# Reordering the edges of a four-stage transformer kernel: weight splits, block boundaries and bank choices

## What is computed

```python
x = x + tanh(g_xattn[0]) * autocorrelation(layernorm(x), ctx, ctx)
x = x + tanh(g_ffn[0]) * lora_ffn(layernorm(x), W, b, A, B, gate_w, gate_b)
x = x + tanh(g_xattn[1]) * attention(layernorm(x), ctx, ctx, mask, wq, wk, wv, wo)
x = x + tanh(g_ffn[1]) * fourier_ffn(layernorm(x), W_base, b_base, enc, coefs, masks)
```

## Time and profile before

| | us |
|---|---|
| median of 3 runs | 3214.91 |
| lowest, highest | 3212.25, 3221.15 |
| the profiled execution, its own time | 3212.81 |
| its span in the trace | 3211.0 |
| TensorE busy in it | 3102.6 |
| VectorE, ScalarE, GpSimd busy | 1940.2, 1136.7, 711.4 |

### The profile page before, as it was taken

One profiled execution on the slowest core, in us unless ns is written; L12 is line 12 of the kernel. 1 busy time (PEld: TensorE's weight loads), 2 busy tenths in 40 slices (PEclk: granted clock), 3 DMA queues, 4 the chain that ended last, 5 costly groups with the idle time before them and its releaser, 6 DMA issues.

```text
span 3211.0 us, 42556 instructions
## 1 busy us (share of the span) xinstructions
PE 3102.6 (97%) x15200; PEld 2594.9 (81%) x15200; DVE 1940.2 (60%) x4647; ACT 1136.7 (35%) x2381; POOL 711.4 (22%) x580
## 2 busy tenths in 40 slices
PE   8999999998899999999999999899999899999999
PEld 7888788886677788887788888788888788888787
DVE  4333487786453577777666667566667566666432
ACT  4111466664222344444333333333333333333221
POOL 2422388884212233332100000000000000000131
PEclk9999999998999999999999999999999999999999
DMA  7332422204352577677564455364455354443621
GB/s 237 128 122 92 153 54 73 71 29 152 112 192 97 189 237 235 224 254 251 175 230 159 152 186 180 120 222 158 158 190 176 126 208 168 163 166 111 255 88 57
DMA packets 232877, 509.67 MB, mean 159 GB/s; under 512 B 23180, under 2 KB 58124, under 8 KB 232668
## 3 DMA queue, kind: packets, MB, share of 16 engines
q1 hardware_dynamic: 231516, 504.14, 46.1%
q10 hardware_dynamic: 1152, 2.82, 0.3%
HBM read 364.29 MB, written 142.61 MB: 158 GB/s over the span
## 4 chain that ended last, share of the span: by engine, by line
PE 64%; DVE 2%; DMA 1%; ACT 1%; issue 1%; POOL 1%; SPq 0%; DVEq 0%; POOLq 0%; ACTq 0%
PE PB L208 52%; PE PB L770 8%; PE PB L1301 3%; PE PB L741 1%; DMA at_wol<-wod 0%; DMA wqd<-at_wql 0%; SPq L119 0%; PE PB L1215 0%; DVE at_hl L196 0%; POOL at_wol L196 0%; ACT at_ss L1282 0%; DVE at_st L213 0%; DVE f0xt L794 0%; DVE at_t L1253 0%; DMA at_rawo<-in_wo 0%
## 5 line engine op out<-in xcount | busy, mean ns | idle before, releaser
L208 PE MATMUL PB<-at_woh,at_ah 128*128 128x512 f32 x1024 | 412.8, 403 | 8.3 <-DMA at_wol<-wod 3.4
L208 PE MATMUL PB<-at_hh,at_wqh 128*128 128x512 f32 x1024 | 401.1, 392 | 3.3 <-DVE at_hl L196 3.3
L208 PE MATMUL PB<-at_woh,at_al 128*128 128x512 f32 x1024 | 401.4, 392 | 0.0
L208 PE MATMUL PB<-at_wol,at_ah 128*128 128x512 f32 x1024 | 401.2, 392 | 0.0
L208 PE MATMUL PB<-at_hl,at_wqh 128*128 128x512 f32 x1024 | 400.7, 391 | 0.0
L208 PE MATMUL PB<-at_hh,at_wql 128*128 128x512 f32 x1024 | 399.7, 390 | 0.0
L1282 ACT ACTIVATE at_ss<-at_ss,at_sm,at_bs 128x256 f32<-128x256 f32 x512 | 301.4, 590 | 263.2 <-DVE at_sm L1280 263.2
L1249 DVE TENSOR_TENSOR at_t<-PB,at_rt 128x512 f32<-128x512 f32 x128 | 88.5, 691 | 441.8 <-PE PB L208 441.8
L1337 DVE SCALAR_TENSOR_TENSOR at_xt<-PB,gt,at_xt 128x512 f32<-128x512 f32 x256 | 191.0, 747 | 130.8 <-PE PB L208 130.8
L193 ACT ACTIVATE at_ah<-PB 128x512 fp32r<-128x512 f32 x128 | 76.7, 599 | 500.7 <-PE PB L208 500.7
L208 PEld LDWEIGHTS PB<-at_woh,at_ah 128*128 128x128 f32 x1024 | 194.0, 189 | 45.3 <-issue 5.4
(11 more groups left out here) (277 smaller groups left out, 7214.7 us busy)
## 6 DMA issues: line engine op xcount, KB each, us to landing
at_wqh<-wqd SPq DMA_DIRECT2D x96, 512.0 KB, 3.6
at_wql<-wqd SPq DMA_DIRECT2D x96, 512.0 KB, 4.5
at_woh<-wod SPq DMA_DIRECT2D x48, 1024.0 KB, 5.1
at_wol<-wod SPq DMA_DIRECT2D x48, 1024.0 KB, 8.0
at_rawq<-in_wq SPq DMA_DIRECT2D x32, 512.0 KB, 4.5
wqd<-at_wqh SPq DMA_DIRECT2D x32, 512.0 KB, 6.1
wqd<-at_wql SPq DMA_DIRECT2D x32, 512.0 KB, 6.8
at_rawo<-in_wo SPq DMA_DIRECT2D x32, 512.0 KB, 7.9
```

What stands on the lines that cost most here:

```text
L208: e.matmul(o, a, b, start=i == 0, stop=last), *(waits if i == 0 else ()), *w, mark=last)
```

## The change

Five groups of edits; no computation is added or left out, but for the engine of four subtractions.

1. In "f0", the splits of weight chunks 4 to 7 are listed after the products of chunks 0 and 1, ahead of the first gates, norms and bias work, where chunks 6 and 7 were split only at c = 4 and c = 5, behind these.
2. In "f0"'s pairs, `ahead(t + 2)` comes before `piece(2t)`, `ahead(t + 3)` after the yield "half" (there, at t = 10, the attention's tile 1 is turned), `lora_in(t + 2)` before `piece(2t + 2)`, and `piece(2t + 3)` before the second `add_lora` and the next gates (for the first pair between the two).
3. `split_wq(n)` for n = 4 to 7 makes its low half on VectorE, where it was on GpSimd.
4. At the end of an attention block, the norms of tiles 0 and 1 move from the start of w = 27 to its end, that of tile 3 from the middle of w = 30 to its end, and the turn of tile 3 from the end of w = 30 into w = 31. `values` at w = 30 goes back to its usual place behind the second output and `weigh`. At w = 31 the two projections of the next block, which stood behind `scores`, come between the two output products.
5. The yield at the end of unit 125 becomes one in unit 126, behind its `fetch_ahead` (which issues `load_wo`); and "f1" turns its tile 1 into `PB[1]` rather than `PB[3]`.

```diff
-                pb = 3 if lora else 2 + s
+                pb = 3 if lora else 1 if t == 1 else 2 + s
...
             split_w(3, *room["w47"])
             for c in range(C):
-                if 2 <= c < C - 2:
-                    split_w(c + 2, *room["w47"])
                 for t in range(2):
                     for hf in range(2):
                         product(t, hf, [c])
                 if c == 0:
                     lora_in(0)
+                if c < 2:
+                    split_w(2 * c + 4, *room["w47"])
+                    split_w(2 * c + 5, *room["w47"])
                 if c == 2:
                     gates_of(0)
...
                     lora_flip(t)
-                if t:
+                    if t + 2 < NT:
+                        ahead(t + 2)
                     piece(2 * t)
-                if t and t + 2 < NT:
-                    ahead(t + 2)
-                if t:
                     product(t, 1)
                 add_lora(t)
...
-                if t and t + 3 < NT:
-                    ahead(t + 3)
...
                 if t:
+                    if t + 3 < NT:
+                        ahead(t + 3)
                     product(t + 1, 0)
-                piece(2 * t + 2)
                 if t + 2 < NT:
                     lora_in(t + 2)
+                piece(2 * t + 2)
...
                     product(t + 1, 1)
+                    piece(2 * t + 3)
                 add_lora(t + 1)
+                if not t:
+                    piece(3)
                 if t + 2 < NT:
                     gates_of(t + 2)
-                piece(2 * t + 3)
...
-                raw_free[0] = wq_of[n] = split(wqh[s][:, :], wql[s][:, :], raw[0][:, :], (raw_of["q"],) + pf, l_on="gpsimd")
+                raw_free[0] = wq_of[n] = split(wqh[s][:, :], wql[s][:, :], raw[0][:, :], (raw_of["q"],) + pf, l_on="gpsimd" if n < 4 or n > 7 else "vector")
...
                 fetch_ahead(u)
+                if u == NU - 2:
+                    yield
...
-                if more and w == 27:
-                    nq = {t: norm(qn + 1, t) for t in range(2)}
...
-                if w == 31 and more:
-                    project(u + 1)()
-                    load_wq(u + 3)
-                rest = project(u + 2) if u + 2 < NU and not late else None
+                last = w == 31 and more
+                rest = project(u + 2) if u + 2 < NU and not late and not last else None
...
-                if late:
-                    nq[3] = norm(qn + 1, 3)
+                if last:
+                    flip(qn + 1, 3, 0, nq[3])
+                    flip(qn + 1, 3, 1, nq[3])
                 if n:
                     output(n - 1, 2 * k)
+                if last:
+                    project(u + 1)()
+                    load_wq(u + 3)
+                    project(u + 2)()
...
-                if u in (NU,) or late:
+                if u == NU:
                     values(u - 1)
...
-                if 4 <= u < NU and not late:
+                if 4 <= u < NU:
                     values(u - 1)
-                if late:
-                    flip(qn + 1, 3, 0, nq[3])
-                    flip(qn + 1, 3, 1, nq[3])
                 split_ahead(u)
-                if more and w == 29:
-                    nq[2] = norm(qn + 1, 2)
-                if u in (NU - 3, NU - 1, NU, NU + 1):
+                if more and w == 27:
+                    nq = {t: norm(qn + 1, t) for t in range(2)}
+                if more and w in (29, 30):
+                    nq[w - 27] = norm(qn + 1, w - 27)
+                if u in (NU - 1, NU, NU + 1):
                     yield
```

## The result

| | us |
|---|---|
| median of before, in the same comparison | 3213.58 (4 runs, 3211.53 to 3221.15) |
| median of after | 3188.89 (4 runs, 3186.33 to 3190.82) |
| ratio, with its 95% interval | 0.9918 (0.9900 to 0.9937) |
| the profiled execution of after, its span | 3187.3, 3185.5 |

24.7 us faster (3213.58 - 3188.89); 3189.4 was forecast. The sum came out, but not all of its terms: the start of the gated layer gave nothing where 3.5 was forecast, and the boundaries gave more than their 13.5.

A forecast was written before the change was run, and what follows sets the result against it. TensorE was taken as the bound, busy 3102.6 of 3211.0 us, leaving waits and low clock to recover. 13.5 + 3.5 + 4.5 - 2.5 + 6.5 = 25.5 us gave a median of 3189.4, forecast range 3181 to 3198 (0.56), 8-in-10 range 3172 to 3205.

The forecast's parts named there:

- Boundaries, 13.5: At three attention block ends, edit 4 replaces the 8.45 us wait by shorter ones: 4.5 us gained each, 13.5 (6 to 24).
- The rival that the wait only moves: At block ends, tile 3's wait lowers the clock and projections wait longer, so edit 4 nets nothing: 3202.9 us; chance 0.13.
- that the waits hide in full: Rival at block ends: waits of 10.6 us and 3 for the clock all vanish, 13.6 each: 3162 us; chance 0.07.
- Start of the gated layer, 3.5: At the start of "f0", edits 1 and 2 bring the first full product 4.0 us earlier, less 0.5 for clock: 3.5 (0 to 8).
- Later pairs, 4.5: In later pairs of "f0", edit 2 removes or shortens waits around `piece`, the turn and "half": 4.5 us gained (1.5 to 7).
- Edit 3, -2.5: At the attention's start, VectorE's subtractions stand ahead of row maxima, rotary step and q: 2.5 us lost (-6 to +3).
- The rival on sharing: In early attention units, ending VectorE's contention with GpSimd makes edit 3 gain 3.1 us instead of losing 2.5: 3183.8; chance 0.14.
- End, 6.5: At the attention's end, edit 5 removes the 3.37 and 1.60 us waits and 1.7 of slow matmuls: 6.5 (4 to 8).
- Sum, 25.5: Whole kernel: all five terms together gain 25.5 us, giving a median of 3189.4 us.

The follow-up runs named there:

- e1: Kernel before with edit 4 alone (the block-end reordering), the yield left where it was; 3197.35 us, 0.9944 of before.
- e2: Kernel before with edit 1 alone (weight chunks 4 to 7 of the gated layer split early); 3206.57 us, 0.9976 of before.
- e3: Kernel before with edit 2 alone (new order in the gated layer's pairs); 3213.84 us, 0.9996 of before.
- e5: Kernel before with only the moved yield of edit 5; from a score behind the third boundary to the last matmul 598.2 us, for 603.3 in before.
- e8: e4 with tile 3's statistics made earlier at a block's end and the exponentials of w = 31 issued later; 3169.11 us.
- e7: e4 with the gated layer's first pair back in before's order: piece(2) ahead of lora_in, piece(3) behind the gates; 3183.09 us.
- e4: Kernel after with edit 3 undone (low halves of query weights 4 to 7 on GpSimd again); 3181.72 us.
- e13: e4 plus the changes of e7 and e8, with GpSimd's first bias additions moved behind the norm of tile 4; 3162.95 us, 0.9841 of before.
- e9: Kernel after with edit 3 doubled (low halves of query weights 4 to 11 on VectorE); 3190.10 us.

## Why the prediction was right, and where not

- **Boundaries, 13.5: right in mechanism, too small.** 15.2 by the median of e1, 17.3 by its D. From the first matmul of `scores` at w = 20 to that at w = 4 of the next block, e1 takes 250.9, 246.2 and 246.2 at the three boundaries; four executions of before's code (before, e2, e3, e5) take 255.6 to 259.4, 251.1 to 252.3 and 251.0 to 251.6. So the second and third gain 4.9 to 6.1, little more than the 4.5 forecast, and the first 4.7 to 8.6. It was mis-sized most: its wait of 3.08, counted as half moved, falls to 0.80, though its turn of tile 3 waits 4.36. Forecast for the second were waits of 1.9, 3.6 and 1.5 and 0.8 for the clock; measured are 1.65 and 3.20. The 1.5 did not come as a wait: turn and first output took 5.4 at the low clock (2010.13 to 2015.56), where 3.5 was counted, and covered it. The rival that the wait only moves falls by e1; that the waits hide in full falls too, though e8's order takes 4.0 more away.
- **Start of the gated layer, 3.5: the step that failed.** A is 55.0 to 56.1 in five executions of this code, 53.6 to 55.4 in three of before's. Tile 3's turn waits 5.5 and `lora_in` 4.2, as forecast (4.6 and 4.7), and the load of `piece(3)` shows 2.45 (3.3). But I priced `lora_in` ahead of `piece(2)` as a gain, put 0.5 on the clock, and put nothing here on the gates, which stand behind `piece(3)` now and need its bank. That order costs 4.3: 0.7 because `piece(3)` starts later behind the turn, 3.6 from its start to the full product (low clock, and the wait of 1.38). It takes about what edit 1 gives, 4 to 6. The rest of the 6.4 between after and e2 (55.8 against 49.4) is, for 1.8 of 2.1, the second bias row (4.50 for 2.73), which is chance. e7 puts both steps of the order back at once, so how much each costs is not shown.
- **Later pairs, 4.5:** measured 5.4 to 6.1. The sum of B's waits fell from 14.83 to 10.42: the 1.05 for the load and the 1.59 behind "half" went, and the waits under 1 fell from 4.6 to 2.7. The wait of 4.24 stayed at 4.34; that about 1 of it goes was wrong.
- **Edit 3, -2.5:** right in sign and in mechanism, too small. C is 3.8 longer than before's, 77.2 against 73.4 on average, and undoing the edit alone gives 6.6 in C and 7.2 in the time. The traces show two parts that the forecast did not have: the subtractions of 1.3 took 2.27 and 1.60 where GpSimd split output weights beside them, and in e4 the 128x4 product (below) met GpSimd once, for 0.62, which before's execution paid with 2.07. All five executions of before's code met it once or twice, for 2.07 to 2.38, and their C is 72.9 to 74.2; e4, e7 and e8, with 0.62 at most, have 70.5 to 72.0. So the edit costs 3 to 4 beside the first and 5 to 7 beside the second. The rival on sharing had the effect right, and its balance wrong: VectorE shares with the output weights instead. The Trainium skill, "SBUF — State Buffer", section "Who interferes with whom", has the rule (a VectorE instruction with two SBUF inputs contends with a GpSimd instruction that reads SBUF); the 2.27 for 1.23 agrees.
- **End, 6.5:** 6.4; 5.1 for the yield (4.9 to 5.1 expected, one run), 1.3 for the bank.
- **Sum, 25.5:** the profiled executions differ by 25.5 as well (3212.81 and 3187.3). Some 2 to 4 too little at the boundaries and 1 in the pairs stand against 4 too much at the start and 1 too little for edit 3's cost. And 1.25 of the 25.5 lie ahead of "f0", where nothing was changed: its first product starts at 767.56 for 768.81. So the agreement to a microsecond is luck, and no proof of the terms.

What is open: why the clock stays low longer behind the same waits in B and C when A is shorter (e7), and why the small product meets GpSimd in some executions and not in others. No run here was made for either question.

## What to carry to other kernels

Price a moved step by the chain that hangs on it, and by what comes to stand behind it: a piece of side work is worth putting where the engine waits anyway, and put behind that wait, with the next step behind it in need of its bank, it cost 4.3 us here. A wait for statistics is often a wait for a place in two lists, and goes when the few small steps are put in the order of their due times (e8: 12.6 us for some moved lines). And test terms one by one: edits of which one gives 4 to 6 and the other costs 4 look like nothing together.

## What the runs showed of the hardware

A small VectorE instruction stood for most of a GpSimd one. In e2, VectorE and GpSimd:

```profile
1111.53 2.07 DVE L1281 TENSOR_TENSOR at_sm<-at_sm,at_nb 128x4 f32<-128x4 f32 x1
...
1122.32 2.27 DVE L1281 TENSOR_TENSOR at_sm<-at_sm,at_nb 128x4 f32<-128x4 f32 x1
```

```profile
1111.19 2.40 POOL L196 TENSOR_TENSOR at_wql<-at_rawq,at_wqh 128x1024 fp32r<-128x1024 f32 x1
...
1122.18 2.39 POOL L196 TENSOR_TENSOR at_wql<-at_rawq,at_wqh 128x1024 fp32r<-128x1024 f32 x1 [0.15 <-ACT at_wqh L193]
```

It ends at 1113.60 and 1124.59, GpSimd's at 1113.59 and 1124.57; alone it takes 0.16. An instruction with one SBUF input was held up too: the 64x1024 row of after took 4.50 beside an addition and two memsets, the same row 2.71 in the kernel before, where the first memset let it pass and took 1.50, and 0.69 alone in e13. Which of these it is changes between executions of the same code: e2 and e8 have 2.73 and 2.71, after and e9 4.50.
